# Seven block products for one corner of tiles 4 and 5, in a fused gated attention and low-rank block on one core

## The reference

```python
def fake_quant(x, scale, zp):
    q = jnp.clip(jnp.round(x / s + z), 0, 255)
    return (q - z) * s
x = x + tanh(g_xattn) * (fake_quant(layernorm(x)) @ fake_quant(ctx))
weight = U * S[None, :] @ V.T
x = x + tanh(g_ffn) * einsum('bti,oi->bto', layernorm(x), weight)
```

## Time and profile before

| | |
|---|---|
| Median of 3 runs | 588.49 us (588.17 to 588.62) |
| The profiled execution | 588.34 us, span 586.5 us |
| TensorE busy | 568.5 us (97%), 2688 matmuls |
| VectorE busy | 447.4 us (76%) |
| ScalarE busy | 235.0 us (40%) |
| GpSimd busy | 196.0 us (33%) |

### The profile page before, as it was taken

How to read it: one execution, slowest core, us unless ns; L and a number is a source line. 1 busy time by engine, 2 the same in 40 slices (tenths; PEclk the granted TensorE clock), 3 DMA queues, 4 the chain that set the end, 5 groups by cost and what they waited for, 6 DMA issues and landing times.

```text
span 586.5 us, 7496 instructions
## 1 busy us (share of the span) xinstructions
PE 568.5 (97%) x2688; PEld 259.7 (44%) x2688; DVE 447.4 (76%) x797; ACT 235.0 (40%) x268; POOL 196.0 (33%) x146
## 2 busy tenths in 40 slices
PE   1899999999999999999999999999999999999998
PEld 0344444444444444444444444444444444444444
DVE  6969999997178873678978799789597986898222
ACT  5799888822123413638723611102530135102200
POOL 2989850000406127846541730220044005310000
PEclk9999999999999999999999999999999999999999
DMA  8999985638927797679865263423954087403722
GB/s 274 387 387 387 340 261 134 127 97 166 280 64 220 170 250 189 206 228 389 271 163 159 56 136 62 122 76 63 225 108 141 4 175 165 125 1 68 166 55 107
DMA packets 145940, 102.73 MB, mean 175 GB/s; under 512 B 108784, under 2 KB 109040, under 8 KB 145904
## 3 DMA queue, kind: packets, MB, share of 16 engines
q1 hardware_dynamic: 136912, 84.96, 54.8%
q10 hardware_dynamic: 8992, 17.30, 8.9%
HBM read 58.99 MB, written 16.78 MB: 129 GB/s over the span
## 4 chain that ended last, share of the span: by engine, by line
PE 93%; DMA 2%; DVE 1%; POOL 1%; SPq 1%; issue 1%; DVEq 0%
PE bank L616 23%; PE bank L692 19%; PE bank L661 11%; PE bank L697 9%; PE bank L755 9%; PE bank L760 9%; PE bank L756 9%; PE bank L579 2%; DMA v_hl<-in_ctx_dram 2%; SPq L331 1%; POOL u8r L270 1%; DVE ring L1332 1%; POOL q L279 1%; SPq L341 0%; PE bank L711 0%
## 5 line engine op out<-in xcount | busy, mean ns | idle before, releaser
L285 POOL TENSOR_SCALAR ring<-ring,bvec 128x2048 f32<-128x2048 f32 x16 | 33.4, 2089 | 259.8 <-DVE bvec L1245 259.8
L616 PE MATMUL bank<-q,qT 128*128 128x512 f16 x512 | 118.1, 382 | 0.0
L692 PE MATMUL bank<-v_hl,xT 128*128 128x512 f16 x448 | 101.3, 379 | 0.0
L290 POOL TENSOR_TENSOR ring<-ring,corr 128x512 f32<-128x512 f32 x64 | 88.4, 1413 | 21.8 <-ACT corr L967 20.8
L755 PE MATMUL bank<-u_hl,hbuf 128*128 128x512 f16 x208 | 78.9, 379 | 0.0
L756 PE MATMUL bank<-u_hl,hbuf 128*128 128x512 f16 x208 | 78.8, 379 | 0.0
L279 POOL TENSOR_SCALAR q<-u8r,const 128x1024 f16<-128x1024 uint8 x52 | 66.4, 1290 | 33.9 <-ACT u8r L864 30.5
L616 PEld LDWEIGHTS bank<-q,qT 128*128 128x128 f16 x512 | 50.4, 98 | 61.4 <-issue 1.4
L692 PEld LDWEIGHTS bank<-v_hl,xT 128*128 128x128 f16 x448 | 43.7, 98 | 52.2
L915 ACT ACTIVATE ln<-ln,const 128x1 f32<-128x1 f32 x16 | 4.7, 295 | 143.8 <-DVE ln L1342 143.8
L1416 DVE SCALAR_TENSOR_TENSOR ring<-bank,cy,ring 128x512 f32<-128x512 f32 x63 | 46.2, 744 | 16.7 <-PE bank L760 16.7
(11 more groups left out here) (173 smaller groups left out, 782.7 us busy)
## 6 DMA issues: line engine op xcount, KB each, us to landing
out_dram<-ring SPq DMA_DIRECT2D x63, 256.0 KB, 3.4
ring<-in_x_dram SPq DMA_DIRECT2D x62, 256.0 KB, 4.2
v_hl<-in_ctx_dram SPq DMA_DIRECT2D x26, 512.0 KB, 11.5
stage<-in_ctx_dram ACTq DMA_DIRECT2D x17, 512.0 KB, 5.5
u_hl<-in_L_ffn_V_dram SPq DMA_DIRECT2D x8, 512.0 KB, 11.4
corr<-in_ctx_dram ACTq DMA_DIRECT2D x8, 512.0 KB, 6.0
stage<-in_ctx_dram SPq DMA_DIRECT2D x6, 512.0 KB, 11.4
q<-in_ctx_dram ACTq DMA_DIRECT2D x4, 512.0 KB, 9.3
```

What stands on the lines that cost most here:

```text
L290: nc.gpsimd.tensor_tensor(xq(t, n), xq(t, n), corr[:, n * W:(n + 1) * W], ALU.add).then_inc(x1_pre, 1)
L616: mm = nc.tensor.matmul(unit_bank(t, n)[:, :], qT_of(t)[:, k, :], q2[:, n, k, :], start=(k == 0), stop=(k == KT - 1))
L692: nc.tensor.matmul(h_bank(u)[:, :], x_home(u, g)[:, half, k % 8, :], v_hl[:, k, 0, :], start=(g == 0 and a == 0 and half == 0), stop=False)
```

## The change

For tiles 4 and 5 and the column blocks 2 and 3, the four units of 16 matmuls are replaced by seven products of 8 (`early_product`), in one go behind the units (5, 0) and (5, 1); mm4(2) comes before the units of tile 5 as it did, but behind two units of tile 4 in place of four. VectorE makes the operands in the lent rooms `u8r`, `stage`, `xs`, `xT`, `xn` and `qn`, each operand in passes of 2048 columns (the sums of A in passes of 1024). The new counter `s_unit` is `unit` without the four units that are gone. Since `stage` and `u8r` are lent, ScalarE begins the context stream (`refill(CB)`) only after P6, and `stream(0, 2)` after P7. The bytes of x of tiles 4 to 7 are made by ScalarE. SyncE stores three blocks of tile 1 and issues `h_transpose(2)` ahead of `q_transpose(4)`, loads x of tile 5 right behind it, and issues `q_transpose(6)` ahead of the stores of tile 3. The new semaphores (`e_t1_made` and so on) are left out here.

```diff
@@ -188,6 +195,9 @@
         unit = lambda t, n: G * n + t if t < G else 6 * NQ + MIXED.index((t, n)) if t in (6, 7) else NQ * t + n
+        EARLY = (TB // 2, TB // 2 + 1)
+        s_unit = lambda t, n: unit(t, n) if t < EARLY[0] else NQ * EARLY[0] + 2 * (t - EARLY[0]) + n if t in EARLY else \
+            unit(t, n) - NQ
         part_count = lambda t, h=1: 2 * t + h + 1 if t < G else 2 * G + t - G + 1
@@ -195,7 +205,7 @@
         pool_count = lambda c: c + 1 - dve_count(c)
-        unit_bank = lambda t, n: bank[4 * (n % 2) + t] if t < G else bank[(unit(t, n) - NQ * G) % 3]
+        unit_bank = lambda t, n: bank[4 * (n % 2) + t] if t < G else bank[(s_unit(t, n) - NQ * G) % 3]
         colsum_bank = lambda b, n: bank[4 * (n % 2) + 3] if b == 0 else bank[(0, 1, 3, 4)[n]]
@@ -212,14 +222,15 @@
 
-        S1_END = lambda t: unit(t, NQ - 1) + 1
+        S1_END = lambda t: s_unit(t, NQ - 1) + 1
+        X1_END = lambda t: unit(t, NQ - 1) + 1
 
...
         XN_ACT = (TB,) + tuple(second_of)
-        Q_ACT = range(TB, NT)
+        Q_ACT = range(R, NT)
         AFTER = (TB + 1,) + tuple(second_of)
@@ -235,6 +246,9 @@
         t4_room = xs[:, :, :, :].rearrange("p g a w -> p (g a w)")
+        e_t1, e_t4 = t4_room, t1_room
+        e_t2, e_t3 = t2_room
+        e_bank = lambda k: bank[{P2: 0, P5: 1, P3: 1}.get(k, 2)]
         t_part = lambda room: room.rearrange("p (k w) -> p k w", k=KH)
@@ -275,7 +289,7 @@
                 if b > 0:
-                    pool.wait_ge(s1_done, unit(TB * b - 1, n) + 1)
+                    pool.wait_ge(s1_done, s_unit(TB * b - 1, n) + 1)
                 nc.gpsimd.tensor_scalar(q2_chunk(c), u8r[:, c % NU8, :], C_NC2, 1.0, ALU.add, ALU.mult)\
@@ -349,6 +363,8 @@
                     sp.wait_ge(p_done, 2 * NP * ((t - PAIRS[0][0]) // 2))
+                elif t - 2 in EARLY:
+                    sp.wait_ge(e_done, NP)
                 elif t > G:
@@ -367,6 +383,8 @@
                     sp.wait_ge(mm3_half, 2 * (u - 1) + g + 1)
+                    if u == EARLY[0]:
+                        sp.wait_ge(e_done, P4 + 1)
                 else:
@@ -476,14 +494,20 @@
             x_transpose(3)
+            store(1, 0)
+            store(1, 1)
+            h_transpose(2)
+            store(1, 2)
             q_transpose(4)
-            turn(1)
+            store(1, 3)
+            for n in range(NQ):
+                load_x(5, n)
             q_transpose(5)
...
             x_transpose(4)
+            q_transpose(6)
             for n in range(NQ):
                 store(3, n)
-            q_transpose(6)
             for n in range(NQ):
@@ -594,7 +618,7 @@
             def s1_part(t, n, k0=0, k1=KT):
-                i = unit(t, n)
+                i = s_unit(t, n)
                 if k0 == 0:
@@ -608,6 +632,8 @@
                             pe.wait_ge(x1_ready, i - 2)
+                        if t == EARLY[1] + 1 and n == 0:
+                            pe.wait_ge(e_read, NP)
                         if t == TB and n == 0:
@@ -662,6 +688,42 @@
                 mm.then_inc(p_done, 1)
+
+            def early_product(k):
+                a, b = EARLY
+                left, right = {P1: (a_part(a, 0), b_part(2, 0)), P5: (s_part(0), t_part(e_t1)),
+                               P6: (s_part(1), t_part(e_t2)), P3: (s_part(2), b_part(3, 1)),
+                               P7: (s_part(3), t_part(e_t3)), P2: (a_part(a, 1), b_part(2, 1)),
+                               P4: (a_part(b, 1), t_part(e_t4))}[k]
+                if k == P1:
+                    pe.wait_ge(x1_ready, s_unit(a, 1) + 1)
+                elif k == P2:
+                    pe.wait_ge(x1_ready, s_unit(b, 0) + 1)
+                elif k == P6:
+                    pe.wait_ge(e_s_made, 2)
+                    pe.wait_ge(e_t2_made, 2)
+                    pe.wait_ge(e_read, P1 + 1)
+                elif k == P5:
+                    pe.wait_ge(x1_ready, s_unit(b, 1) + 1)
+                    pe.wait_ge(e_t1_made, 2)
+                elif k == P7:
+                    pe.wait_ge(e_s_made, 4)
+                    pe.wait_ge(e_t3_made, 2)
+                    pe.wait_ge(e_read, P6 + 1)
+                elif k == P3:
+                    pe.wait_ge(e_read, P5 + 1)
+                else:
+                    pe.wait_ge(e_t4_made, 2)
+                    pe.wait_ge(e_read, P7 + 1)
+                for i in range(KH):
+                    mm = nc.tensor.matmul(e_bank(k)[:, :], left[:, i, :], right[:, i, :],
+                                          start=(i == 0 and k in (P1, P2, P5)), stop=(i == KH - 1),
+                                          skip_group_check=k in (P6, P7, P4, P3))
+                mm.then_inc(e_done, 1)
+
+            def early_quad():
+                for k in range(NP):
+                    early_product(k)
 
@@ -812,9 +874,12 @@
             mm3(3)
-            s1(4)
+            s1_part(4, 0)
+            s1_part(4, 1)
             mm4(2)
-            s1(5)
+            s1_part(5, 0)
+            s1_part(5, 1)
+            early_quad()
             mm4(3)
@@ -894,6 +959,10 @@
                 act.wait_ge(qT_in, 16 * (t - G))
+                if t == R:
+                    act.wait_ge(split_lo, VP + RT)
+                if t == EARLY[1] + 1:
+                    act.wait_ge(e_done, P7 + 1)
                 if t == TB:
@@ -1072,34 +1141,39 @@
             root1(4)
+            quantise(4)
             op2(4)
-            act.wait_ge(split_lo, VP + RT * NQ)
+            hid_hi(3)
+            root1(5)
+            quantise(5)
+            op2(5)
+            act.wait_ge(e_t4_made, 2)
+            act.wait_ge(e_done, P6 + 1)
             refill(CB)
             refill(CB + 1)
-            stream(0, 2)
-            root1(5)
-            op2(5)
+            root1(6)
             root2(4)
             x_hi(4)
+            quantise(6)
+            op2(6)
+            act.wait_ge(e_done, P7 + 1)
+            stream(0, 2)
+            root2(5)
+            x_hi_half(5, 0)
+            x_hi_half(5, 1)
+            hid_hi(4)
             stream(2, 4)
-            hid_hi(3)
-            root2(5)
-            root1(6)
-            x_hi_half(5, 0)
-            op2(6)
-            x_hi_half(5, 1)
-            stream(4, 6)
-            hid_hi(4)
             root1(7)
+            quantise(7)
             op2(7)
-            stream(6, 8)
+            stream(4, 8)
             act.wait_ge(xs_lo, 2 * 6)
...
             stream(8, 10)
-            act.wait_ge(x1_pre, S1_END(TB - 1))
+            act.wait_ge(x1_pre, X1_END(TB - 1))
             refill(CB + ORDER.index("corr0"))
@@ -1226,8 +1300,6 @@
                     dve.wait_ge(qT_in, 16 * (t - G))
-                if t == R:
-                    dve.wait_ge(split_lo, VP + RT)
                 if t < G:
@@ -1257,8 +1329,8 @@
             def x1_unit(t, n):
-                i = unit(t, n)
-                dve.wait_ge(x1_pre, i + 1)
+                i = s_unit(t, n)
+                dve.wait_ge(x1_pre, unit(t, n) + 1)
                 dve.wait_ge(s1_done, i + 1)
@@ -1267,6 +1339,57 @@
                     x1_unit(t, n)
+
+            def early_t3():
+                for c in range(2):
+                    b12, b22 = [k_piece(flat2(b_part(3, h)), c, 2 * HW) for h in range(2)]
+                    tt(k_piece(e_t3, c, 2 * HW), b22, b12, ALU.subtract).then_inc(e_t3_made, 1)
+
+            def early_t2():
+                for c in range(2):
+                    dve.wait_ge(e_t3_made, c + 1)
+                    tt(k_piece(e_t2, c, 2 * HW), k_piece(e_t3, c, 2 * HW), k_piece(flat2(b_part(2, 0)), c, 2 * HW),
+                       ALU.add).then_inc(e_t2_made, 1)
+
+            def early_t1():
+                for g in range(2):
+                    dve.wait_ge(xT_in[g], 16 * x_dma(EARLY[0] - 1))
+                for c in range(2):
+                    b11, b12 = [k_piece(flat2(b_part(n, 0)), c, 2 * HW) for n in (2, 3)]
+                    tt(k_piece(e_t1, c, 2 * HW), b12, b11, ALU.subtract).then_inc(e_t1_made, 1)
+
+            def early_t4():
+                dve.wait_ge(mm3_half, 2 * EARLY[0])
+                for c in range(2):
+                    dve.wait_ge(e_t2_made, c + 1)
+                    tt(k_piece(e_t4, c, 2 * HW), k_piece(flat2(b_part(2, 1)), c, 2 * HW), k_piece(e_t2, c, 2 * HW),
+                       ALU.subtract).then_inc(e_t4_made, 1)
+
+            def early_s_sums():
+                a, b = EARLY
+                A11, A12, A21, A22 = [flat2(a_part(t, h)) for t in EARLY for h in range(2)]
+                S1, S2, S4, S3 = s_room
+                dve.wait_ge(qT_in, 16 * (b - G + 1))
+                dve.wait_ge(xs_lo, 2 * a)
+                tt(S1, A21, A22, ALU.add).then_inc(e_s_made, 1)
+                dve.wait_ge(e_s_made, 1)
+                tt(S2, S1, A11, ALU.subtract).then_inc(e_s_made, 1)
+                dve.wait_ge(e_s_made, 2)
+                tt(S3, A11, A21, ALU.subtract).then_inc(e_s_made, 1)
+                tt(S4, A12, S2, ALU.subtract).then_inc(e_s_made, 1)
+
```

(70 more changed lines are left out.)

## The result

| | before | after |
|---|---|---|
| median | 588.43 us (588.17 to 588.62, 4 runs) | 596.65 us (595.93 to 597.26, 4 runs) |
| profiled execution | 588.34 us, span 586.5 | 596.10 us, span 594.3 |
| TensorE | 2688 matmuls | 2680 matmuls |

The ratio is 1.0141 [1.0130, 1.0153]: the change makes the kernel 1.4% slower. The forecast was 588.3, with a range up to 591.2.

The account below looks back on a forecast made before the run. The prediction took the kernel to be bound by TensorE. Its terms, -1.73 for matmuls saved, +0.45 at the products and +1.15 at tile 7's first unit, summed to -0.1 us: 588.3 us, range 586.5 to 591.2.

Parts of the forecast that it names:

- What is taken away: Tiles 4 and 5 on TensorE: 64 matmuls become 56, a gain of 1.73 us if nothing waits.
- Quantising on ScalarE: Both passes on ScalarE, 4.25 us; tile 4's transpose issued at 147.0, landing before it is wanted; cost 0.
- qT(5): Tile 5's quantised transpose, wanted 6.9 us earlier, lands at 169.7, 0.9 before that; cost 0, bounds 0 and 1.5.
- the term for (7,0): Tile 7's first unit: its transpose lands at 229.1 against 227.95; cost 1.15 us, bounds 0 and 2.5.
- P1 to P6: First six products: the sixth waits for VectorE's add of the first until 181.35; cost 0.45 us, bounds 0 and 2.0.
- x of tile 4: Tile 4's x, transpose issued 5.4 us after the last product, covered by mm4(3); cost 0, bounds 0 and 3.5.
- Tile 5's second norm, and tile 7: Tile 5's transpose lands at 217.0, wanted at 217.65, cost 0, bounds 0 and 3; tile 7's first unit costs 1.15.
- The context stream: Stream about 2 us later at 240, taken up by ScalarE's idle time before the root at 253.81; cost 0, bounds 0 and 1.
- The late norm decides: Rival, chance 0.22: tile 5's late root and tile 5 and 7 transposes make TensorE wait; 589.6 to 592 us.

Follow-up runs that it names:

- edit 8: The changed kernel with ScalarE's steps ordered by when they are wanted and the context chunks between them; 589.06 us, ratio 1.0014.
- edit 9: As edit 8, but tile 7's quantising is given back to VectorE; 588.29 us, ratio 1.0002.
- edit 1: The changed kernel with context chunks 2 and 3 and their two refills moved behind tile 7's quantising on ScalarE; 594.11 us, ratio 1.0107.
- edit 11: The kernel before with chunks 4 and 5 and their refills moved behind tile 7's second pass, run once; 588.27 us.
- edit 7: The kernel before, all 2688 matmuls, with only the context stream made as late as the change's; 593.92 us, ratio 1.0110.
- edit 3: The changed kernel with tile 5's two transposes of x ahead of tile 7's loads on SyncE, measured once; 605.02 us.
- edit 2: The changed kernel with tile 5's second root and high halves ahead of the first two context chunks on ScalarE; 592.69 us, ratio 1.0076.
- edit 10: As edit 9, but the two refills behind chunks 2 and 3 are placed behind tile 7's second pass on ScalarE; 594.60 us, ratio 1.0096.
- edit 4: The changed kernel with the reorderings of edit 1 and edit 2 together; 593.08 us, ratio 1.0082.

## Why the prediction was wrong

- **What is taken away** was right: 2680 matmuls, and tile 6's units begin at 210.38 against 212.18, 1.8 us sooner.
- **Quantising on ScalarE, qT(5)**: q_transpose(4) was issued at 146.95 (forecast 147.0). t3 and t2 ended at 154.5 and not at 156.3, since VectorE's first two passes were not stretched. Cost 0, as forecast. (By its own rows four passes at 2.3 in place of 1.22 are 4.3 us of GpSimd's work, not 4.6; nothing hangs on it.) For tile 7, edits 8 and 9 differ by 0.8 us in the median, with intervals that just touch, and their transposes were issued at 222.76 and 221.34: there ScalarE's slower passes seem to lie on the path, as the term for (7,0) had it. Its 1.15 us in the sum could not be read in the change itself, where the longer wait covered it; with edit 9 it is 1.2 with VectorE's passes.
- **P1 to P6** was forecast to cost 0.45 and cost 0. The add of P1 ran from 179.57 to 180.32, where 181.35 was forecast and P6 wanted it at 180.9.
- **x of tile 4** cost 0, as forecast: its first transpose was issued at 194.99, 5.3 us after P4's end, for 5.4 (the addends given, 1.7, 1.2 and 2.1, make 5.0).
- **The step that failed** is the first part of "Tile 5's second norm, and tile 7": "With the median of 5.2 us it lands at 217.0; wanted at 217.65 ... Cost 0, bounds 0 and 3." The issue was right to 0.7 us (212.5 for 211.8). The landing took 12.4 us, so it came at 224.9, and the wait was 7.6. I took the median of all such transposes, when the 9.2 in the earlier trace rows was this very one, behind the same loads and beside refills. With 9.2 the text would have had 221.0 and a wait of 3.4 us, which covers the 1.15 at (7,0), and a forecast of 590.4: still within its range, and 6 us short of the result. The rest is that I never set the refills at 212.3 and 214.0 beside it, though the change puts them there: edits 1 and 11 show that 5.8 to 6.2 us of transfer become 12.4 and 9.2 with refills.
- **A term was missing**: what TensorE does after a wait. A gap of 7.6 us cost 1.8 more at the lower clock.
- **The context stream**, "cost 0, bounds 0 and 1", failed too: edit 7, a stream as late in the kernel before, costs 5.5 us in the median (4.6 to 8.3 by its interval), though its trace shows only 2.6. I looked for the delay at the root at 253.81, where there is room, and not at what is queued behind the chunks before that (hid_hi(5), root2(6)), nor at the transposes beside their refills.
- **The late norm decides**, a rival at 0.22, named the place and the chain, and its sign was right: VectorE stood idle for 4.8 us (6 by the text), and the transpose of tile 7 was issued at 226.04, after the 224.5 that it gave as its condition. Its price, "up to 2 us" at mm3(5) and 589.6 to 592 in all, fell short by the same transfer time and by the missing clock.

## What to carry to other kernels

Take the landing of a transfer from the row with the same neighbours in flight, not from the median, and when a stream of work is moved, set each transfer it issues against each urgent one of that time. On an engine that works in order, list every step that stands behind the moved stream, since the delay lands on the last of them and moves on when that one is brought forward. A saving ahead of a chain that runs at its own pace (loads, norm, transpose of the next tile) is only had if the chain starts earlier too.

## What the runs showed of the hardware

**Transposes beside loads.** The same transpose took 4.4 us with no load ahead of it and the first refill 1.7 us behind (edit 3), 5.8 behind 1 MB of loads (edit 1), and 11.2 to 12.4 behind the loads and beside two to four refills of 512 KB as well (the change, edits 7 and 2). The table by stage shows 180 to 192 GB/s moved in that time at a DMA share over 1, so the DMA engines were occupied throughout. A transfer behind a pass in an engine's order can leave while that pass still runs (edit 10).

**The clock.** After a wait of 7.6 us 16 matmuls took 5.39 us, after 4.5 5.30, where 3.62 is their time. Waits of 1.2 and 1.6 (edits 1 and 7) cost nothing more. Around 2.3 it went either way: 1.7 us were lost in edits 1, 4 and 8 (2.2 to 2.4 us of wait), none in edit 10, whose 96 matmuls took 20.89 us after a wait of 2.44.

**Who is held off.** In the earlier trace rows VectorE and GpSimd stretched each other. Here, in GpSimd's and VectorE's timelines of the change:

```profile
147.34 3.85 POOL L299 TENSOR_SCALAR ring<-ring,bvec 128x2048 f32<-128x2048 f32 x1 [65.68 <-DVE bvec L1317]
```

```profile
147.09 2.35 DVE L1346 TENSOR_TENSOR u8r<-q 128x2048 f16<-128x2048 f16 x2
149.36 5.12 DVE L1351 TENSOR_TENSOR stage<-u8r,q 128x2048 f16<-128x2048 f16 x2
```

VectorE's first two passes ran at full pace (2.35 us for both), and GpSimd's took 3.85 in place of 1.97: counted back from its end at 151.19, its own 1.97 began at 149.2, as VectorE's second pass ended. VectorE's next two took 5.12, the first of them 2.91: it ended at 152.27, 1.1 us after GpSimd's pass. The same happened at 165.0 (2.35 us, GpSimd's 3.94). So twice GpSimd stood still behind two passes of VectorE, where I had each give way in turn.
By the Trainium skill (SBUF — State Buffer, section "SBUF: two separate sides") the port is an exclusive lock for a whole instruction, and the trace agrees with the lock; that the waiting engine comes next, as the prediction read it, it does not bear out.
